# Selective-state-space layer with butterfly FFN: first butterfly stage as diagonal products, first outputs issued sooner, contraction products in two pairs

## The reference, cut to what matters

```python
x = x + ssm(layernorm(x))
x = x + ffn(layernorm(x))

def ssm(x):                                  # d_inner 512, 16 states
    x_inner, z = split(x @ in_proj_w.T)
    x_conv = silu(causal_conv4(x_inner) + conv_b)
    delta, B, C = softplus(x_dbl[..., 0]), ...           # x_dbl = x_conv @ x_proj_w.T, 33 columns
    h = h * exp(delta * A) + x_conv * (delta * B)        # a scan over the tokens
    y = (h . C + x_conv * D) * silu(z)
    return y @ out_proj_w.T

def ffn(x):                                  # hidden 1024
    h = x @ W_exp + b_exp
    h = butterfly(h, up_weights)             # 10 stages; stage s pairs i with i ^ 2**s by a 2x2 matrix each
    h = gelu(h + up_bias)
    h = butterfly(h, down_weights)           # 10 stages
    return h @ W_con + b_con + down_bias
```

## Time and profile before

| | |
|---|---|
| median of 3 runs | 543.27 us |
| the profiled execution | 543.8 us, of which the span 542.1 us |
| PE busy | 516.0 us (95%) |
| DVE busy | 416.8 us (77%) |
| ACT busy | 307.0 us (57%) |
| POOL busy | 93.3 us (17%) |
| mean granted clock of PE | 0.981 |

### The profile page before, as it was taken

How to read it: one execution, slowest core, us unless ns; L and a number is a source line. 1 busy time by engine, 2 the same in 40 slices (tenths; PEclk the granted TensorE clock), 3 DMA queues, 4 the chain that set the end, 5 groups by cost and what they waited for, 6 DMA issues and landing times.

```text
span 542.1 us, 8227 instructions
## 1 busy us (share of the span) xinstructions
PE 516.0 (95%) x3012; PEld 422.5 (78%) x3012; DVE 416.8 (77%) x892; ACT 307.0 (57%) x537; POOL 93.3 (17%) x88
## 2 busy tenths in 40 slices
PE   4989999998999999999999999999999999889997
PEld 3756776776887788878888788888888789578886
DVE  4778999888984999489975999489956986576542
ACT  2777883794249622875269722964278514951242
POOL 4040200220211202140211211030213021122020
PEclk9995988999999999999999999999999999999999
DMA  9652511200112001210112002110021001200011
GB/s 223 134 28 3 83 39 41 66 16 2 39 40 76 6 2 50 69 41 1 40 40 81 0 2 79 54 28 2 0 79 42 1 1 39 81 0 1 1 40 39
DMA packets 42635, 21.75 MB, mean 40 GB/s; under 512 B 26435, under 2 KB 41027, under 8 KB 42596
## 3 DMA queue, kind: packets, MB, share of 16 engines
q1 hardware_dynamic: 39956, 17.57, 13.9%
q10 hardware_dynamic: 2640, 3.67, 2.4%
HBM read 16.78 MB, written 4.46 MB: 39 GB/s over the span
## 4 chain that ended last, share of the span: by engine, by line
PE 58%; DVE 20%; ACT 9%; issue 9%; POOL 2%; DMA 1%; DVEq 0%; ACTq 0%; POOLq 0%
PE wide L715 11%; PE acc L877 11%; PE wide L866 9%; PE wide L855 9%; DVE xc L1516 5%; PE wide L829 4%; DVE state L1621 3%; PE small L705 3%; PE wide L840 2%; ACT xc L1186 2%; DVE diag_sum L1639 2%; DVE diag L1635 2%; DVE hid_low L1533 1%; PE wide L725 1%; PE small L735 1%
## 5 line engine op out<-in xcount | busy, mean ns | idle before, releaser
L1146 ACT ACTIVATE hid_f<-wide,bias_up 128x512 f32<-128x512 f32 x64 | 43.9, 686 | 160.5 <-PE wide L866 157.5
L1516 DVE SCALAR_TENSOR_TENSOR xc<-xi,taps,xc 128x512 f32<-128x512 f32 x96 | 96.2, 1007 | 4.5 <-ACT xc L1177 2.3
L877 PE MATMUL acc<-w_down_high,hid_high 128*128 128x256 f32 x256 | 73.7, 288 | 3.5 <-DVE hid_low L1533 3.4
L877 PE MATMUL acc<-w_down_high,hid_low 128*128 128x256 f32 x256 | 72.0, 281 | 0.0
L877 PE MATMUL acc<-w_down_low,hid_high 128*128 128x256 f32 x256 | 72.0, 281 | 0.0
L1533 DVE TENSOR_TENSOR hid_low<-hid_f,hid_high 128x512 fp32r<-128x512 f32 x64 | 47.4, 743 | 15.5 <-ACT hid_high L1259 15.2
L855 PE MATMUL wide<-w_out,xc 128*128 128x256 f32 x256 | 58.4, 388 | 0.7 <-DVE xc L1660 0.5
L715 PE MATMUL wide<-xnT_ln1T_high,w_in_high 128*128 128x512 f32 x128 | 56.7, 443 | 0.0
L877 PEld LDWEIGHTS acc<-w_down_high,hid_high 128*128 128x128 f32 x256 | 48.3, 188 | 10.2 <-issue 6.6
L866 PE MATMUL wide<-xnT_ln2T_high,w_up_high 128*128 128x512 f32 x128 | 54.2, 424 | 1.7 <-DVE xnT_ln2T_low L1527 1.7
L855 PEld LDWEIGHTS wide<-w_out,xc 128*128 128x128 f32 x256 | 49.2, 194 | 7.8 <-issue 1.1
(11 more groups left out here) (193 smaller groups left out, 1035.3 us busy)
## 6 DMA issues: line engine op xcount, KB each, us to landing
x_res<-in_L_attn_x_dram SPq DMA_DIRECT2D x9, 512.0 KB, 3.5
c_near<-c_of_tokens SPq DMA_DIRECT2D x8, 512.0 KB
x_ln<-in_L_attn_x_dram SPq DMA_DIRECT2D x7, 512.0 KB, 3.6
out_dram<-x1b_xn SPq DMA_DIRECT2D x7, 512.0 KB, 2.9
xc<-in_L_attn_in_proj_w_dram ACTq DMA_DIRECT2D x2, 512.0 KB, 7.1
xc<-in_L_ffn_W_exp_dram ACTq DMA_DIRECT2D x1, 1024.0 KB, 11.1
x1b_xn<-in_L_ffn_W_con_dram ACTq DMA_DIRECT2D x1, 1024.0 KB, 15.0
raw_out<-n_L_attn_out_proj_w_dram ACTq DMA_DIRECT2D x1, 512.0 KB, 7.7
```

Of the source, the lines that this page charges most:

```text
L877: last = pe.matmul(acc[:, c, :], hid[h][:, j % HRING, c * P:(c + 1) * P], w_down[w][:, j, 0:DM], start=j == 0 and c % 2 == 0 and n == 0, s ...
L1146: ins = act.activation(out_ap, in_ap, how.pop("func"), **how)
L1516: ins = dve.scalar_tensor_tensor(xc[u % BATCH][:, e, :], xi[:, e, tap:tap + TILE], taps[:, e, tap:tap + 1], xc[u % BATCH][:, e, :], ALU.mu ...
```

## The change

- The first high stage of the up butterfly (stage 7) leaves ACT and DVE. POOL spreads the 8 x 2 weight columns of stage 7 over diagonal matrices `diags` (one `affine_select` of 128 x 2048 elements; the view is 16 matrices of 128 x 128), and `pathT` multiplies each block of `paths` with a diagonal matrix in place of the identity: 16 float32 products in four results (steps 8 and 9) where 8 transposes in two stood. `up_low` then sums two products for each block: 16 where 8 stood. `MIXES[UP]` has two stages left. `pathT` now lies in the `low_w` tensor of the up butterfly and no longer in `x_res`.
- The three small loads of the up butterfly's high weights go ahead of `x_res` and of the 14 loads of `low_w` in SP's queue.
- DVE's wait for POOL's last zeroing moves from `constants()` to the middle of `softplus(0)`.
- `silu(z)` of unit 0 is done in two halves (`silu_first_z`), the first right after the last z copy of unit 0, the second after `prepare(13)`.
- PE's first phase: `off_diagonal(0)` and the first y pair come before input product 6 of unit 1, the second y pair before input product 7, the first output product before the products of `prepare(15)` and the transposes of unit 2.
- DVE's first phase: the four gates come right after `advance_state(0)`; the paths of the down butterfly come after them; `add_blocks(UP, 0)` stands between `second_stats(0)` and `second_normalise(0)`, after both residuals.
- Phase 1: `add_blocks(UP, 1)` (was 2) stays at its place; the low parts of `w_up` and of `w_down` are split in pairs around `convolve(2, 0)`, `sum_diagonal(1)` and `assemble(1)`; PE makes the first two `w_down` products before the first `up` product, and ACT copies them before the gelu table is loaded.

```diff
-    WIDE_ORDER += uses(("xp", [0]), of=phase) + uses(("in", range(8)), of=phase + 1)
+    WIDE_ORDER += uses(("xp", [0]), of=phase)
...
+    if phase == 0:
+        WIDE_ORDER += uses(("in", range(6)), of=1) + uses(("y", range(2)), of=0)
+        WIDE_ORDER += uses(("in", [6]), of=1) + uses(("y", range(2, CB)), of=0)
+        WIDE_ORDER += uses(("in", [7]), of=1) + uses(("out", range(2)), of=0)
...
-        pathT = x_res[:, :, :].rearrange(flat).rearrange("p (g j) -> p g j", j=P)
+        pathT = low_w[0][:, :].rearrange("p (n j) -> p n j", j=P)
+        diags = mixed[:, :, :].rearrange(flat)[:, 0:2 * HID].rearrange("p (n j) -> p n j", j=P)
...
             [("pathT", 0, 0), ("pathT", 1, 0)],
+            [("pathT", 2, 0), ("pathT", 3, 0)],
...
-            [("w_down", q, 0) for q in range(4)],
+            [("w_down", q, 0) for q in range(2)],
+            [("w_down", q, 0) for q in range(2, 4)],
...
-        MIXES = {UP: [(0, mixed, wexpT), (1, wexpT, mixed), (2, mixed, wexpT)],
+        MIXES = {UP: [(1, mixed, wexpT), (2, wexpT, mixed)],
...
+            load_high(UP, high_loaded)
             sp.dma_start(x_res[:, :, :], tokens(1)).then_inc(early_loaded, 16)
             load_low(sp, UP, up_weights)
...
+            def weights_on_diagonals(stage):
+                pool.affine_select(out=diags, in_=high_w[UP][:, stage, :, :].rearrange("p q w -> p (q w)").unsqueeze(2)
+                                   .to_broadcast([P, 2 * HB, P]), compare_op=ALU.is_equal, fill=0.0, base=0,
+                                   pattern=[[0, 2 * HB], [-1, P]], channel_multiplier=1).then_inc(diags_made, 1)
+            pool.wait_ge(high_loaded, 16 * HIGH)
+            weights_on_diagonals(0)
             rstd_of(1, 0, var1, rstd1)
...
-                        last = pe.transpose(bank[:, q * P:(q + 1) * P], paths[UP][:, g * P:(g + 1) * P], ident[:, :])
+                        n = 4 * i + q
+                        g = n // 4 * 2 + n % 2
+                        last = pe.matmul(bank[:, q * P:(q + 1) * P], paths[UP][:, g * P:(g + 1) * P], diags[:, n, :],
+                                         start=True, stop=True)
...
-                    last = pe.matmul(bank[:, 0:W1], pathT[:, i, :], wexpT[:, i, :], start=True, stop=True)
+                    for n in range(2):
+                        last = pe.matmul(bank[:, 0:W1], pathT[:, 2 * i + n, :], wexpT[:, i // 2 * 2 + n, :],
+                                         start=n == 0, stop=n == 1)
...
+            def silu_first_z(h):
+                read(act, 0, "in", 2 * h + 5)
+                half = slice(2 * h, 2 * h + 2)
+                act.activation(z[0][:, half, :], z[0][:, half, :], ACT.Silu).then_inc(first_z_ready, 1)
...
                 elif place == "products":
+                    prepare(18)
                     wait_all_taken("w_up")
                 elif place == "up 1":
-                    prepare(17)
+                    prepare(19)
```

More of the change, by code:

```diff
@@ L78 @@
     some_ups = lambda many: uses(("up", list(islice(ups, many))), of=phase - 1)
-    WIDE_ORDER += some_ups(first) + uses(("y", range(2)), of=phase)
-    WIDE_ORDER += some_ups(between) + uses(("y", range(2, CB)), of=phase)
-    WIDE_ORDER += some_ups(then) + uses(("out", range(2)), of=phase)
-    WIDE_ORDER += some_ups(HB)
+    if phase == 0:
+        WIDE_ORDER += uses(("in", range(6)), of=1) + uses(("y", range(2)), of=0)
+        WIDE_ORDER += uses(("in", [6]), of=1) + uses(("y", range(2, CB)), of=0)
+        WIDE_ORDER += uses(("in", [7]), of=1) + uses(("out", range(2)), of=0)
+    else:
+        WIDE_ORDER += uses(("in", range(8)), of=phase + 1)
+        WIDE_ORDER += some_ups(first) + uses(("y", range(2)), of=phase)
+        WIDE_ORDER += some_ups(between) + uses(("y", range(2, CB)), of=phase)
+        WIDE_ORDER += some_ups(then) + uses(("out", range(2)), of=phase)
+        WIDE_ORDER += some_ups(HB)
     SMALL_ORDER += uses(("xtok", range(GR)), ("xdtok", [0]), of=phase)
@@ L449, in _, with load_high @@
             sp.dma_start(raw_x, x_proj_w).then_inc(w_loaded["x_proj"], 16)
+            def load_high(i, signal):
+                for s in range(HIGH):
+                    sp.dma_start(high_w[i][:, s, :, :], (up_weights, down_weights)[i][LOW + s].rearrange("(q p) o i -> p q (o i)", p=P)).then_inc(signal, 16)
+            load_high(UP, high_loaded)
             sp.dma_start(x_res[:, :, :], tokens(1)).then_inc(early_loaded, 16)
@@ L469, in load_for_residual @@
                 if u == 0:
-                    sp.wait_ge(made, number[("up_low", HB - 1, 0)] + 1)
+                    wait(sp, norm1, 1, GR)
                 sp.dma_start(x_res[:, :, :], tokens(u)).then_inc(res_loaded.handle, 16)
@@ L666, in make @@
                         pe.wait_ge(s_loaded, 16 * SMALL_LOADS)
-                        wait_taken(pe, ("pathT", 0, 0))
-                        wait_taken(pe, ("pathT", 1, 0))
-                    last = pe.matmul(bank[:, 0:W1], pathT[:, i, :], wexpT[:, i, :], start=True, stop=True)
+                        for q in range(4):
+                            wait_taken(pe, ("pathT", q, 0))
+                    for n in range(2):
+                        last = pe.matmul(bank[:, 0:W1], pathT[:, 2 * i + n, :], wexpT[:, i // 2 * 2 + n, :],
+                                         start=n == 0, stop=n == 1)
                 elif name == "w_up":
-                    wait_mixed(pe, UP, HIGH - 1, HB - 1)
+                    wait_mixed(pe, UP, 1, HB - 1)
                     for q in range(4):
-                        last = pe.transpose(bank[:, q * P:(q + 1) * P], wexpT[:, 4 * h + q, i * P:(i + 1) * P], ident[:, :])
+                        last = pe.transpose(bank[:, q * P:(q + 1) * P], mixed[:, 4 * h + q, i * P:(i + 1) * P], ident[:, :])
                 else:
@@ L797, in off_diagonal, with ssm_output @@
                 mark_written(last, "moff", 0, u)
-            def ssm_output(u):
-                for pair in ((0, 1), (2, 3)):
+            def ssm_output(u, pairs=((0, 1), (2, 3))):
+                for pair in pairs:
                     for g in pair:
@@ L1341, in phase @@
                     copy_z(v, 7)
+                beside("z 7")
                 copy_first_state(u)
@@ L1361, in weights_of_ffn @@
                 if place == "ln2T":
-                    scale_blocks(UP, 2)
+                    scale_blocks(UP, 1)
                 elif place == "z 5":
-                    prepare(15)
+                    prepare(16)
                 elif place == "z 6":
-                    prepare(16)
+                    prepare(17)
+                elif place == "z 7":
+                    prepare(18)
                 elif place == "gelu 1":
-                    prepare(17)
+                    prepare(19)
             prepare(0)
@@ L1665, in gates_of_halves @@
                 if pair == 0:
-                    wait(dve, z_ready, u, 1)
+                    wait(dve, z_ready, u - 1, 1)
                 for h in range(2):
@@ L1763, in to_first_outputs @@
                 convolve(v, 0)
+                beside("convolved")
                 diagonal_times_c(u)
                 sum_diagonal(u)
+                beside("diagonal")
                 assemble(u)
@@ L1859, in weights_of_ffn @@
                 if place == "softplus":
-                    add_blocks(UP, 2)
+                    add_blocks(UP, 1)
                 elif place == "weighed":
-                    low_of_ffn(("w_up", 0, 0), ("w_up", 0, 1), ("w_up", 1, 0), ("w_up", 1, 1))
+                    low_of_ffn(("w_up", 0, 0), ("w_up", 0, 1))
+                elif place == "convolved":
+                    low_of_ffn(("w_up", 1, 0), ("w_up", 1, 1))
+                elif place == "diagonal":
+                    low_of_ffn(("w_down", 0, 0), ("w_down", 1, 0))
                 elif place == "assembled":
-                    low_of_ffn(*(("w_down", q, 0) for q in range(4)))
+                    low_of_ffn(("w_down", 2, 0), ("w_down", 3, 0))
             wait(dve, ln_loaded, 0, 16)
```

64 lines of the change are left out of this document (36 added, 28 removed).

## The result

In six runs of each on one chip the kernel before took 543.79 us (543.27 to 544.44) and the changed one 547.78 us (545.88 to 548.83): a ratio of 1.0076, 95% interval 1.0066 to 1.0085. So it is slower by 4.0 us; 547.2 was forecast. The profiled execution of the changed kernel took 548.75 us, of which the span is 547.0, against 543.8 and 542.1.

The account below looks back on a forecast made before the run. PE bounds the kernel (busy 95%), with DVE pacing it from 58 to 87 us. 0.7 + 0.3 + 0.6 + 2.3 = +3.9 on the profiled 543.8 gives 547.7, median 547.2; 8-in-10 range 543.0 to 550.2.

Parts of the forecast that it names:

- Sum: Whole kernel: +3.9 us, from 0.7 added products, 0.3 loads, 0.6 clock and 2.3 for DVE and phase 1.
- T: When PE finishes unit 0's output products, before at 96.11: 96.8 from added products alone, +1.6 with loads and clock.
- the loads: Three high loads ahead of the 14 low ones on SP: later by 0 to 2.6 us, taken as 0.3.
- Clock behind low products: Each of three series of few-row products has half clock behind it; 0 to 3.3 us return, taken as 0.6.
- Clock, by the page: Skill page's rule: real products replacing 8 transposes keep PE's clock up, so the 0.6 becomes 0, sum 546.6.
- Gates: End of phase 0: last gate at 84.0 against 87.21, first output product more than 2 us behind, lead unused.
- Phase 1 up to `c_start`: Normalisation done 8.65 after T instead of 6.0; PE waits 1.2 for unit 0's tokens; `c_start` 2.65 late.
- The pairs: Split low parts in phase 1: convolution held 1.6, waits of 1.00 and part of 0.71 gone; 2.65 becomes 2.3.
- POOL and zeroing: `affine_select` takes 0 to 5 us in POOL's pause, costed at nothing; the freed wait for zeroing gains nothing.
- 1 (the lead carries through): Rival: added products fit PE's hidden pauses, T at 93.0, -2.1, 541.2; decided if T under about 95; chance 0.10.
- 2: Rival, no change: T at 96.1, DVE's added work half absorbed; 0 to +1, 543.8; chance 0.14.
- Rival 3: Much slower: PE's waits bring another half-clock stretch, loads cost 2.6; +8.9 at most, about 551; chance 0.10.

Follow-up runs that it names:

- full rows: Low products of the down butterfly read 128 rows, contraction weights left out: changed kernel 1.0044; with blocks and low parts early 0.9987; kernel before 1.0008.
- blocks early: Changed kernel with the 8 instructions of `add_blocks(UP, 0)` moved into DVE's pause ahead of the residuals, and ACT's `scale_blocks` sooner: 546.11 us, ratio 1.0039.
- the output first: Changed kernel with the first half of the output product ahead of both low steps of the down butterfly: 551.55 us, ratio 1.0143.
- blocks and low parts early: Changed kernel with `add_blocks(UP, 0)` in DVE's pause and unit 2's low parts between the two residuals: 544.77 us, ratio 1.0025.

## Why the prediction was right, step by step

- **Sum.** Forecast +3.9 and 547.2; measured +4.0 and 547.78. Sign and mechanism held, and so did the size in the median. The profiled execution, one of the slower ones, lost 4.9: 1.7 in T, 2.6 from there to `c_start`, 0.2 won by the pairs, and 0.8 behind the first contraction product. The forecast had 1.6, 2.65, 0.35 won, and nothing for the last. Inside T two terms were mis-sized in opposite directions.
- **T.** Forecast +1.6 as 0.7 for PE's added products, 0.3 for the loads and 0.6 for the clock; measured +1.7. Of this the clock is 1.8 by itself in the profiled execution (5.41 - 3.62), so added products and loads came to nothing where 1.0 was forecast. The list of items is the first error. From the first products with the state to the low products it counts 8.8 us (75.37 to 84.2); the rows have 8.1 (75.23 to 83.34), since products set side by side took 0.2 to 0.3 less than the pieces summed. The loads show no cost: PE's start on the low products of the up butterfly (36.84, 37.47 in the earlier trace rows) still waits 0.81 for ACT, and it lies between 36.2 and 37.7 in the ten profiles with the new order of loads, between 36.2 and 38.2 in the four with the old. The clock is the second error: 0.6 was taken since dense products surround the low ones, but they didn't protect the output products. In the median it is nearer to 1.2 (the pair with few and full rows). That T came out is partly luck.
- **Clock behind low products.** Of the four series of low products in the changed kernel (36.84, 45.29, 83.34, 91.40) only the first and the third have half clock behind them. And in the profile of the kernel before with the pairs alone the output products ran at full clock (7.15 for what took 8.83), with the same products in front. So the stretch behind each of three series that the prediction read off one trace is not a rule.
- **Clock, by the page.** The products in place of transposes began in the profile after a wait of 2.53 and ran at half clock: 3.45 for the first sixteen records, 1.95 for the second. The Trainium skill, TensorE: Matmul & The Clock Gate, Part 4: PE-mode transpose, would have had real products keep the clock up and made T 0.6 sooner; neither this nor the 5.41 agrees with that use of it. The rule itself, on transposes, isn't refuted: here waits and low products stood beside them. The 3.45 cost nothing further on: with the blocks early the same sixteen took 1.95 without a wait, and the y blocks began at 73.41 there and at 73.45 here, where PE has to wait for `m_mat` in any case.
- **Gates.** The last one ended at 84.11 (84.0 forecast), the first output product came 1.95 behind (more than 2 forecast): the lead was used by nobody. The run with the output first shows that using it is worse.
- **Phase 1 up to `c_start`.** The normalisation ended 8.6 behind T (8.65), PE's waits for unit 0's transposes came to 1.1 (1.2), `c_start` at T + 19.5 against T + 16.9 (+2.6; +2.65 forecast). The two runs with the blocks moved, one from each kernel, and the one with the low parts show it: 2.0 to 2.8 of the 4.0 us are this order.
- **The pairs.** 0.35 forecast, 0.2 in the profile, 0 in the median. The 0.35 doesn't follow from its own terms: 1.6 for the held convolution against waits of 1.00 and 0.71 leaves 0.1 at most. The convolution was held by 1.2, and the runs with phase 1 as before and with the pairs alone show that this was not on the path. The error was to count the wait of 1.00 as won: what PE waits for next is a chain of ACT and DVE that comes at its own time. With the pairs, ACT loads its gelu table behind the first copies of `w_down`, makes two gelus and their high parts, and only then the last copies, for which DVE waits 2.37 (rows below, with POOL's product). By the Trainium skill, SBUF — State Buffer, SBUF: two separate sides, the price was up to 2.4, for a whole instruction. The trace agrees with a hold for what was left of POOL's product: it ran from 118.79 to 121.19, the convolution came at 119.82 with 1.4 of it left, and one of its three instructions took 1.92 where the two others took 0.75.

```profile
127.41 1.28 ACT L1246 ACT_TABLE_LOAD   x1
...
131.29 1.07 ACT L1139 ACTIVATE w_down_high<-acc 128x512 fp32r<-128x512 f32 x2
```

```profile
118.79 2.40 POOL L621 TENSOR_TENSOR c_near<-c_near,dB 128x1024 f32<-128x1024 f32 x1
```

- **POOL and zeroing.** The `affine_select` of 2048 elements took 2.01 us (0 to 5 allowed) in a pause, as this row of POOL's timeline shows. POOL then waited 10.85 for its next work, and no later row shows a cost; no run leaves out this instruction alone:

```profile
15.59 2.01 POOL L576 TENSOR_SCALAR_AFFINE_SELECT mixed<-high_w 128x2048 f32<-128x2048 f32 x1 [2.35 <-DMA high_w<-in_L_ffn_up_weights_dram]
```

- **Rivals.** 1 (the lead carries through) fell with the first output products: T would have to be under 95.5. Of the profiles with the new order it is under that only with full rows: 95.09 with DVE's order as changed, and that kernel is still slower (1.0044); 95.10 with DVE's order mended, and that one is level or faster (0.9987). 2 is out by the interval. 3 was half there: a wait at the diagonal products and half clock at 134.7 to 137.6, but no more than 0.8 of the span. That stretch is the prediction's own sign "if the clock stays low elsewhere", so this sign did show, in a small size. (Rival 3's +8.9 would be 552.2, not 551.)
- **What stays open.** What makes the clock fall at the output products in one execution and not in the next. Full rows in the low products brought 2.0 us in the median in the new order, of which about 1.2 may be clock; in the old order an earlier T is not used, so nothing can be read there; and moving the low products away by one input product shows nothing in the median. T itself is no clean measure of it: with phase 1 as before it is 97.87 in the profile, though the first half of the output products took 3.72, since there the y blocks began at 75.22. No version with all of its work beat the kernel before; the nearest are the pairs alone (1.0000) and the blocks and low parts early (1.0025).

## What to carry to other kernels

Before moving work off an engine, ask whether it lay in a pause: sixteen instructions of DVE beside PE's output products were free, and the eight that remained, set behind the point at which PE hands over, cost 1.4 to 2.0 us. They were free only as long as PE came no sooner: where PE handed over 1.5 us earlier, they kept DVE from using it. Take each handover between two engines as a clock of its own (here "so much behind T"): if the receiving engine has no slack there, every instruction put ahead of the token is paid in full. And judge two parts of a change together as well as apart: here one filled the wait that the other made.

## What the runs showed of the hardware beyond that

- One program has executions with and without a stretch of half clock at the same place. The changed kernel's six runs spread over 2.95 us, the kernel before's 1.2; with blocks and low parts early it is 3.4 and with full rows 1.5. The same 16 records of output products, with the same products of PE in front, took 5.41 in two profiles (the changed kernel; blocks and low parts early) and 3.72 in two others (blocks early; phase 1 as before).
- The six low products of one step, whose operands have 4 to 128 rows (x12 in the rows, named there by one of their shapes), took 2.73 to the next instruction's start, with 128 rows for all 2.18, at full clock both.
- Half clock stood behind these waits of PE: 5.95 before the y blocks (3.75 for records that take 1.95) and 2.77 before the last y blocks. A wait of 1.78 to 1.79 before the contraction has it in some profiles and not in others. Of the nine profiles with the pairs, the changed kernel's and three more have 0.66 as the mean clock over the 5 us behind that wait, the other five 1.00. From the first contraction product to the end the four took 413.1 to 413.3 us, the five 412.2 to 412.5.
